# Edge pass of a graph network: the attention vector of two VectorE multiplies moves from SBUF to PSUM

## The reference

```
i, j = edge_index[0], edge_index[1]
out_i = softplus(concat([x[i], edge_attr], -1) @ W).reshape(-1, 4, 64)
out_j = softplus(concat([x[j], edge_attr], -1) @ W).reshape(-1, 4, 64)
alpha = softplus((concat([out_i, out_j], -1) * att).sum(-1))
# batch norm of alpha over the edges, softplus, softmax over the edges of a node i
out = segment_sum(out_j * alpha[:, :, None], i).mean(1) + bias
```

## Time and profile before

| what | value |
|---|---|
| median of 3 runs | 17978.42 us (17961.65 to 17998.12) |
| the profiled execution | 17943.85 us, its span 17941.9 us |
| busy shares of the span | PE 42%, PEld 28%, DVE 37%, ACT 29%, POOL 45% |
| edge pass, first to last L1009 | 546.4 to 7683.1 us of the span, 202 groups |

### The profile page before, as it was taken

How to read it: one execution, slowest core, us unless ns; L and a number is a source line. 1 busy time by engine, 2 the same in 40 slices (tenths; PEclk the granted TensorE clock), 3 DMA queues, 4 the chain that set the end, 5 groups by cost and what they waited for, 6 DMA issues and landing times. The chain is left out here.

```text
span 17941.9 us, 161975 instructions
## 1 busy us (share of the span) xinstructions
PE 7458.8 (42%) x27414; PEld 5083.7 (28%) x27414; DVE 6696.2 (37%) x15251; ACT 5174.2 (29%) x11311; POOL 8096.2 (45%) x8196
## 2 busy tenths in 40 slices
PE   4554454454554544400012550873332343233357
PEld 3333232332332323300002550232222232222223
DVE  5555555555555555542112771011111121111111
ACT  0233333333333333310112661023333333333310
POOL 0444444444444444447775006016666636666600
PEclk9777777777777777755555565985555565555578
DMA  1333333333333333350112551751111131111136
GB/s 24 88 98 96 96 95 95 99 94 96 99 94 96 95 95 98 93 26 22 30 32 73 184 182 33 255 191 22 22 22 22 22 102 22 22 22 22 21 132 223
DMA packets 1037233, 1461.80 MB, mean 81 GB/s; under 512 B 518414, under 2 KB 733934, under 8 KB 1011937
## 3 DMA queue, kind: packets, MB, share of 16 engines
q1 hardware_dynamic: 651986, 1075.95, 19.3%
q0 software_dynamic: 284800, 382.51, 8.8%
q10 hardware_dynamic: 100368, 2.41, 0.7%
HBM read 946.06 MB, written 512.36 MB: 81 GB/s over the span
## 5 line engine op out<-in xcount | busy, mean ns | idle before, releaser
L1533 POOL DMA_INDIRECT l2s_got<-rel_d,l2s_idx x3232 | 3073.2, 951 | 2680.8 <-POOLq L1530 1727.1
L793 POOL DMA_INDIRECT rows_d<-edge_rows,edge_place x1624 | 1675.2, 1032 | 3439.2 <-POOLq L791 2987.2
L1559 PE MATMUL l2s_ps<-l2s_got,l2s_oh 128*128 128x65 f32 (+1 forms) x6464 | 1473.3, 421 | 3403.7 <-PEq L1557 2754.1
L1559 PEld LDWEIGHTS l2s_ps<-l2s_got,l2s_oh 128*128 128x128 f32 x6464 | 1409.0, 330 | 3469.3 <-issue 3469.3
L873 PE MATMUL edge_z<-edge_w,edge_feats 128*128 128x512 f32 x3232 | 2049.8, 721 | 599.5 <-PEq L870 581.7
L1231 DVE TENSOR_TENSOR net_acc<-net_acc,l2s_ps 128x65 f32 (+1 forms) x3232 | 719.3, 223 | 4147.5 <-issue 3701.7
L886 PE MATMUL edge_at<-edge_upto,edge_oh_loT 128*128 128x50 f32 x3232 | 697.8, 303 | 3002.9 <-PEq L885 1721.2
L1249 POOL DMA_INDIRECT count_d<-all_list_val,all_list_idx x1568 | 1680.2, 1072 | 563.1 <-issue 467.5
L785 POOL DMA_INDIRECT edge_gath<-h_d,edge_idx x1624 | 1592.0, 980 | 501.0 <-issue 494.4
L950 DVE SCALAR_TENSOR_TENSOR edge_prod<-edge_soft,edge_z 128x512 f32<-128x512 f32 x808 | 552.8, 684 | 3030.7 <-DVEq L949 2693.1
L1362 PE MATMUL at_ps<-at_msg,at_oh 128*128 128x128 f32 x3520 | 762.9, 405 | 1951.2 <-PEq L1358 737.8
(11 more groups left out here) (367 smaller groups left out, 10651.5 us busy)
## 6 DMA issues: line engine op xcount, KB each, us to landing
at_rows<-rows_d SPq DMA_DIRECT2D x444, 528.0 KB
count_d<-edge_zero SPq DMA_DIRECT2D x202, 994.0 KB
l1s_cnt<-count_d SPq DMA_DIRECT2D x49, 1600.0 KB, 6.4
l3s_cnt<-count_d SPq DMA_DIRECT2D x49, 1600.0 KB, 6.4
rel_d<-l2t_out SPq DMA_DIRECT2D x100, 768.0 KB, 3.3
l1s_cnt<-count_d SPq DMA_DIRECT2D x49, 1536.0 KB, 6.1
l3s_cnt<-count_d SPq DMA_DIRECT2D x49, 1536.0 KB, 6.0
edge_drow<-loc_d SPq DMA_DIRECT2D x203, 256.0 KB
```

The source lines that it names most:

```text
L793: pool.indirect_dma_start(out=net.rows_d, out_offset=bass.IndirectOffsetOnAxis(ap=place[q][:, j:j + 1], axis=0), in_=rows[q][:, j, :], in_ ...
L1533: pool.indirect_dma_start(out=got[r][:, j, 0:cols], out_offset=None, in_=table, in_offset=bass.IndirectOffsetOnAxis(ap=idx[i][:, k:k + 1], ...
L1559: ins = pe.matmul(ps[q][:, j, 0:wide], oh[q][:, j, :], got[r][:, j, 0:wide], start=True, stop=True)
```

## The change

One PSUM tile `att_ps` of the shape of `att` is added (2 KB a partition, the eighth bank). Before the loop VectorE copies `att` into it once and waits for the copy. L957 and L961 read `att_ps` in place of `att`. `att` is otherwise used nowhere.

```diff
@@ -709,6 +709,7 @@
     nxt = e.ps("nxt", [P, 512])
+    att_ps = e.ps("att_ps", [P, 2, OUTJ])
@@ -730,7 +731,7 @@
-    values_made = sem("values_made")
+    values_made, att_kept = sem("values_made"), sem("att_kept")
@@ -954,12 +955,12 @@
-                v.tensor_tensor(prod[:, :, 0:OUTJ], prod[:, :, 0:OUTJ], att[:, 0:1, :].to_broadcast([P, 2, OUTJ]),
+                v.tensor_tensor(prod[:, :, 0:OUTJ], prod[:, :, 0:OUTJ], att_ps[:, 0:1, :].to_broadcast([P, 2, OUTJ]),
                                 ALU.mult)
                 v.wait_ge(out_j_made, 1).then_inc(out_j_made, -1)
                 v.sem_inc(z_free, 1)
                 v.tensor_tensor(prod[:, :, OUTJ:WIDE], rows[q][:, tiles, 0:OUTJ],
-                                att[:, 1:2, :].to_broadcast([P, 2, OUTJ]), ALU.mult).then_inc(multiplied, 1)
+                                att_ps[:, 1:2, :].to_broadcast([P, 2, OUTJ]), ALU.mult).then_inc(multiplied, 1)
@@ -978,6 +979,8 @@
             v.wait_ge(weights_loaded, 16 * 4)
+            v.tensor_copy(att_ps[:, :, :], att[:, :, :]).then_inc(att_kept, 1)
+            v.wait_ge(att_kept, 1)
```

## The result

The changed kernel takes 17999.6 us (median of 17 runs, 17959.8 to 18030.0), the kernel before 17970.8 (17 runs, 17929.9 to 18000.3): a ratio of 1.0017, with a 95% interval of 1.0010 to 1.0025. That is +29 us, where the prediction said +117. In two later comparisons the same pair gave 1.0023 (1.0008 to 1.0038) and 1.0010 (0.9997 to 1.0023). So the change costs some 0.1 to 0.2%, and the third comparison alone does not tell it from nothing.

What follows compares the result with a forecast made beforehand. No engine was taken as the bound: POOL's burst delays messages, then VectorE sets some 11 us. Copy and PSUM operand 0, lost pauses +1.18 x 101 = +119 us on 17978, rounded to 18095 us; range 17885 to 18220.

Steps and rivals of the forecast that it cites:

- Steps 1 and 2: Edge pass: the single copy costs below 1 us, taken as 0; reading PSUM adds 0 ns to each of 1616 multiplies.
- the 52 us: Edge pass multiplies: the addition if a PSUM input costs 65 ns more per instruction, by the skill's fixed cycles.
- the 331 us by L994's row: Edge pass multiplies: upper end if PSUM operands cost 0.41 us more each; rival "PSUM operand is slow", 18309 us, chance 0.04.
- step 3: GpSimd scatters: VectorE's multiplies stop holding them; most of 0.42 us a group goes, mean of L793 below 0.99 us.
- Step 4: Edge groups: without pauses messages come later; +0.78 and +0.40 us for the two kinds, 1.18 x 101 = +119 us; chance 0.45.
- late: Edge group where save 6 comes only after POOL's burst, at 24.3 us; it takes 36.71 us against a normal 35.76.
- the second kind: Edge groups in which ACT does not reload its table, 97 of 193; forecast to go from 35.28 to 35.68 us, +0.40.
- this case: Edge pass: the phase of p = 0 settles elsewhere, so L927 or the one-hot instructions make a new pause; no size given.
- fast groups: Edge groups where save 7 comes before the burst ends, at 20.8 us, taking 32.07 us; forecast to be gone.
- The burst sets the end: Rival, edge groups: save 7 stays tied to the last gather, groups shrink 0.46 us, 93 us in all, 17885 us; chance 0.22.
- All late: Rival, edge groups: without any pause both kinds go to 36.7 us, +232 us in all, 18210 us; chance 0.12.
- Nothing moves: Rival, edge groups: one shared path always in use, pauses only move work about, 17978 us; chance 0.17.

Runs made afterwards that it cites:

- e5: The changed kernel, unmodified, timed again beside the kernel before (17951.6 us): 17993.8 us, ratio 1.0023.
- e13: The changed kernel, unmodified, timed once more beside the kernel before (17977.1 us): 17987.4 us, ratio 1.0010.
- e15: Half the change on the kernel before: only the second multiply (L962) reads PSUM, long condition (groups of 35.5 us): 18022.4 us, ratio 1.0018.
- e6: The kernel before, unmodified, run once more for its profile in the long condition: 17963.6 us.
- e14: Changed kernel plus a small GpSimd instruction and wait in front of each group's first scatter, before the burst: 17917.6 us, ratio 0.9970.
- e7: Changed kernel plus a GpSimd instruction and wait, a 0.88 us pause, in front of each group's third scatter: 17396.8 us, ratio 0.9682.
- e16: The kernel before plus a 0.88 us GpSimd pause in front of each group's third scatter: 17341.4 us, ratio 0.9645.
- e19: Changed kernel plus seven 0.88 us GpSimd pauses, at scatters 3, 5, 7 and gathers 1, 3, 5, 7: 16287.4 us, ratio 0.9072.
- e18: Changed kernel plus a shorter GpSimd pause (8 columns, 0.68 us) in front of each group's third scatter: 17065.3 us, ratio 0.9503.
- e4: Half the change on the kernel before: only the second multiply (L962) reads PSUM, short condition (kernel before 13334.6 us): 13330.1 us, ratio 0.9996.
- e8: Half the change on the kernel before: only the first multiply (L958) reads PSUM, long condition: 17894.3 us, ratio 0.9963.

## Why the prediction was wrong

**Steps 1 and 2 held.** The copy took 685 ns once. The multiplies with a PSUM input took 678 ns, L951 beside them 683, so the 52 us by the Trainium skill's page (VectorE: DVE Perf Modes, the errata section) and the 331 us by L994's row are both out.

**Step 3 held for what it named and missed the rest.** No third scatter is held in any of the 193 groups. But step 3 went on to say that most of VectorE's 0.42 us a group goes. The mean of L793 was forecast below 990 ns and is 1026. In the profile before 355 of the 363 scatters that took over 1.04 us had started under L957 or L961, and only one under L927 or L932. In the profile after there are still 233, and 131 of them started under L928 or L933 (the same two instructions), 56 under L962 with L928 beginning before they ended.

**Step 4 is where it failed, and by size.** Its mechanism was right: where a group falls in the old phase and has no pause, it is late. In the profile after four groups of the first kind (those in which ACT reloads its table behind tail(3)) have p = 0 at 1.69 to 1.79 us and two are late; in e5 three of five, in e13 nine of nine, in e15 sixteen of eighteen, the last two with a mean of 36.75 and 36.66 us. Before, with the pause, it was one of nineteen, at 34.71, and none of 22 in e6. The term took the +0.78 and +0.40 us of today's groups without a pause for those of all groups. But of the 31 such groups of the first kind 27 have p = 0 at 1.79 us or later, where no other instruction made up for the pause, and of the 16 of the second kind six have the multiply's pause at the fourth scatter instead (1.23 to 1.40 us). Neither set stands for all phases. Two things went otherwise. The first needs no shift: at the phase of 1.1 to 1.6 us a pause at the seventh and eighth scatter took the place of the one that went, as the group at 2820.78 us against the one at 2930.74 us shows. With the phases of the profile before and the mean lengths that the three profiles of the changed kernel have at each phase, the first kind would have gone up by 0.38 us, half of the 0.78. The second is that phases did not stay as they were. In the first kind, 58 of 96 groups now have p = 0 at 1.1 to 1.6 us (22 before), where L928 and the one-hot instructions of src_hots meet the last scatters, and those take 35.55 us in the mean. The first kind went up by 0.11 us instead of 0.78, the second by 0.30 instead of 0.40. Together that is 0.41 us a pass and 41 us instead of 119 in the profile, and 29 in the medians. The prediction had named this case last among what would make it wrong, and gave it neither a price nor a chance. Why the phase settles there is not shown. Of its other signs, the zero write at 16 us and more came true (17.1 us in the mean). The wait in front of L951 grew by 0.3 us a group and not by 0.6, the fast groups did not go (16, after 18), and 23 of the 96 groups of the first kind are late, not most. A fast group is followed by one with p = 0 at some 3.2 us, which is late (2962.70, 37.54 us), so lengths of neighbours hang together.

**The rivals.** "The burst sets the end" is out: e14 delays the burst, e7 and e16 to e19 lengthen it by 0.7 to 6.2 us, all in the long condition, and all six are faster. "All late" is out at +29 us. "Nothing moves" gave 17978 and comes nearest in size, but its reason, that pauses only move work about, is refuted by e7 and e18. So its nearness is luck: pauses that went and pauses that came nearly cancel here.

**What stays open.** What SP's, ACT's and PE's instructions and messages share with GpSimd's descriptor generation was not found, nor why two conditions exist. That groups with more pause are shorter is a count over seven profiles, and the written pauses bear it out in direction but not in proportion (0.68 us gave more than 0.88). Why the changed kernel, with about the same sum of pauses, has more late groups is open: no run pauses at the seventh or eighth scatter alone, and none keeps L928 and L933 away from them.

## What to carry to other kernels

When an instruction stops interfering with another, ask which of its neighbours will meet it next, and whether the phases shift too; a term sorted out of today's groups holds only for the phases that those groups have. Before counting a collision as loss, see who is served during the stall: here a pause of 0.7 us in GpSimd's burst bought 4.3 us a group (e18, 31.2 us against 35.5). And where a kernel's time differs by a third between chips, time a change in both conditions: a pause worth 5% in one costs 0.25% in the other.

## What the runs showed of the hardware

The same kernel took 13.33 ms on two chips and 17.95 to 17.98 ms on others, with nothing in between. What differs is the edge pass, from 35.5 to 21.6 us a group (before; e4), and the stages after it, from 10259 to 8450 us. In the short condition the messages do arrive during the burst. The timeline of e4, a group from 3007.85 us whose end is at 3030.12:

```profile
3007.85 0.19 DVE L1012 TENSOR_TENSOR edge_rows<-edge_dots 128x32 f32<-128x32 f32 x1
...
3014.14 0.63 SPq L772 DMA_DIRECT2D count_d<-edge_zero  x1
...
3015.46 1.02 ACT L829 ACTIVATE edge_soft<-edge_z 128x1024 f32<-128x1024 f32 x1 [2.18 <-ACTq L840]
...
3016.38 0.20 ACT L819 COPY edge_upto<-edge_nxt 128x49 f32<-128x49 f32 x1
...
3018.83 0.20 ACT L819 COPY edge_upto<-edge_nxt 128x49 f32<-128x49 f32 x1 [2.26 <-ACTq L818]
```

Save 7 comes at 11.0 us, with GpSimd's burst at its eighth scatter, where the same message comes behind the sixteenth in the long condition.

A DMA_INDIRECT of GpSimd that starts while VectorE runs a multiply with two SBUF inputs waits for it (0.96 us becomes up to 1.48). It can also be held beside L928, a one-input tensor_scalar (1.30), and beside L933, which has two SBUF inputs, and what follows it (1.72). With one SBUF and one PSUM input it isn't: of the 225 scatters that start under L958 in the profile after none takes over 0.99 us, and the 56 that start under L962 and take up to 1.33 are those during which L928 begins. The Trainium skill (SBUF — State Buffer, Who interferes with whom) infers for tensor_tensor that it does not hold up descriptor generation; the rows of L957, L961 and L933 disagree.

Who waits is settled within some 10 to 30 ns. A scatter (nearly always the eighth) that starts at most 0.03 us behind L932 (L933 in the changed kernels) either takes 0.96 us, and then the VectorE instruction takes 0.73 to 0.75, or that one takes 0.67 to 0.69, and the scatter some 1.72. Held are 1 of 70 and 3 of 74 such scatters in the two profiles of the kernel before, 3 of 59 in e15, and 64 of 77, 60 of 62, 59 of 63 and 79 of 79 in the three of the changed kernel and in e8.
